# Two-layer transformer on one core: first-layer output products from split operands, reordered heads, later second-layer weights

## The chip, the cores and the metric

One core of one Trainium2 chip. The time is microseconds of device time from launch to end; of a kernel several executions are taken and the median stands for it. One more execution is profiled, and all rows come from that.

## What is computed

Two layers over 8 batches of 512 tokens with 128 features. In each layer attention and a feed-forward part both read the normalised rows, and both are added to the input. What matters here, cut from the reference:

```python
# layer 0, attention: 16 heads of 64 (x is normalised, 8 x 512 x 128)
y = jnp.einsum('bhcC,bhCv->bhcv', p, v)              # p: causal softmax
z = jnp.einsum('dvh,bhcv->bcd', W, y) * (math.sqrt(d_embed / d_value) / num_heads)
# layer 0, feed-forward: 32 routed experts (6 per token) and a shared one
hmid = jax.nn.silu(gate) * up
out = jnp.einsum('teh,te->th', y, combine) + shared_out
# layer 1, feed-forward: three blocks of two linear layers
w = q.astype(jnp.float32) / 7.5 - 1.0
w = w * jnp.repeat(scale, GROUP, axis=1)
base = jnp.einsum('btd,od->bto', x, w) + bias
lora = jnp.einsum('btr,or->bto', jnp.einsum('btd,rd->btr', x, la), lb)
return base + lora
```

## The kernel before

**Tiling.** Tokens of a batch are four tiles of 128; a product's moving operand has 512 columns. Many products are made in fp32r, a single-pass format: an operand is split in a high part (a rounded copy) and a low part (value minus high part), and `split_matmul` (lines 61 to 66) makes three products of them (high-high, high-low, low-high) in place of one fp32 product. Projections, scores, expert units and their down products are made so. The attention's output products (`project_out`, line 1703) are plain fp32 on `w_out0` and `yt`, eight per batch, one for each pair of heads, summed in PSUM bank 7 with the down products of the 17 units.

**Stages.** For batches 0 to 7: eight slots of attention, one for each pair of heads (`slot`, `score_group`), then 17 units (`units`: unit 0 is the shared expert, the others are two routed experts each). Within the units of batch b the rows, router logits, first projections and values of batch b + 1 are made. Where batch b's units end and batch b + 1's first slot begins stands `first_head`: the last down products, the output products of batch b and the first scores of batch b + 1. This stretch, up to the first turned blocks, is called a head below; there are seven, the first one after batch 0. After batch 7 comes layer 1 in two groups of four batches.

**A unit.** TensorE makes gate and up (bank pairs alternate), ScalarE the SiLU (`silu`, line 879), VectorE multiplies by the up half in PSUM (`gate`, line 1293; it frees the banks) and by the routing weights (`hidden`, line 1303, both operands in SBUF; the weights come by DMA to `crow`, three deep), ScalarE makes the high part (line 869), and VectorE (line 1297) or GpSimd (line 592) the low part (high part and value both in SBUF). For units 14, 15 and 16 it is VectorE. The down product of unit u follows the projection of unit u + 3. In batches 1 to 6 VectorE has layer 1's row statistics in unit 14.

**Other work of GpSimd.** `divide_pair` (line 588) multiplies `yt` by the inverse softmax sums, which SyncE fetches to `rrow` (two DMAs a pair). The two last pairs come behind the low part of unit 13. In batch 0, `second_layer_weights` dequantises layer 1's weights behind that.

**Order.** Each engine has its own queue, written out by hand; nothing is scheduled at run time but the semaphore waits. SyncE issues all DMAs from one queue, and waits in it for free buffers. The LoRA products (`add_lora`, line 1550) stand in unit 16 of batch 0; their operands are fetched in unit 2 of it, ScalarE copies them out of PSUM and GpSimd adds the rest.

Of the kernel before, what the change touches and what calls it, by code (L numbers as in the profile page):

```python
# [5 lines left out]
F32 = mybir.dt.float32  # L6
# [8 lines left out]
P = 128  # L15
# [8 lines left out]
R, GROUP, NLIN = 32, 16, 6  # L24
BLOCKS = NLIN // 2
# [56 lines left out]
def build(nc, a, out_dram):  # L82
    with ExitStack() as ctx:
# [17 lines left out]
        wqkv_rest = sb("wqkv_rest", [P, 2 * 3 * PAIRS * P - 2 * TILES * TILES * P])  # L101
        with ExitStack() as raw:
# [3 lines left out]
        w_out0 = sb("w_out0", [P, PAIRS, D])  # L106
# [11 lines left out]
        lin = sb("lin", [P, NLIN, D])  # L118
# [33 lines left out]
        rrow = sb("rrow", [P, RROWS, T])  # L152
        pt = sb("pt", [P, 2, TILES, TILES, P])
        yt = sb("yt", [P, PAIRS, T])
# [13 lines left out]
        hm_hi = [qk_hi[:, 1, 0, :], qk_hi[:, 1, 1, :], hm_third[:, 0, :]]  # L168
        hm_lo = [qk_lo[:, 1, 0, :], qk_lo[:, 1, 1, :], hm_third[:, 1, :]]
# [27 lines left out]


# [6 lines left out]
        la, lb = (flat_pt[0:R, k * NLIN * D:(k + 1) * NLIN * D].rearrange("p (n d) -> p n d", n=NLIN) for k in (0, 1))  # L205
        lora = lin[:, :, :].rearrange("p i o -> p (i o)")
# [106 lines left out]
        lora_taken = sem("lora_taken")  # L313
# [41 lines left out]
        y_divided = sem("y_divided")  # L355
        y_done = sem("y_done")
# [80 lines left out]
        SUMS_AFTER = [2, 3, 4, 8, 9, 10, 12, 13]  # L437
# [12 lines left out]
        LORA_AFTER = 16  # L450
# [14 lines left out]
        lora_loads = [(la, a["la"]), (lb, a["lb"])]  # L465
# [5 lines left out]
        def _(sp):  # L471
# [40 lines left out]
            for b in range(B):  # L512
# [6 lines left out]
                for u in range(2, UNITS):  # L519
# [4 lines left out]
                    if b == 0:  # L524
                        sp.wait_ge(y_done, PAIRS)
                        if u == 2:
                            for dst, src in lora_loads:
                                sp.dma_start(dst, src).then_inc(lora_loaded, 16)
                if b == 0:
                    sp.wait_ge(hm_ready, UNITS - 1)  # L530
                    sp.wait_ge(y_divided, PAIRS)
                    for dst, src in w1_loads:
                        sp.dma_start(dst, src).then_inc(w1_loaded, 16)
                    sp.wait_ge(lin_ready, 1)
# [10 lines left out]
        def _(pool):  # L545
# [58 lines left out]

            def split_gu(k):
# [18 lines left out]
            def second_layer_weights():  # L624
# [4 lines left out]
                setup.step(pool.tensor_tensor(wf, wf, qs, ALU.mult))  # L629
                pool.wait_ge(lora_taken, 2)  # L630
                pool.tensor_tensor(lin[:, :, :], lin[:, :, :], wf, ALU.add).then_inc(lin_ready, 1)
# [22 lines left out]
            for k in range(len(DOWN_PIECES)):  # L654
                split_down(k)
# [1648 lines left out]
```

## Time and profile before

| what | value |
|---|---|
| median of 3 runs | 1170.06 us (1169.66 to 1171.59) |
| the profiled execution | 1168.83 us |
| its span (first to last instruction) | 1167.0 us |
| busy: TensorE, VectorE, ScalarE, GpSimd | 99%, 85%, 70%, 35% |
| mean granted TensorE clock | 1.000 of full speed |
| chain that ended last | TensorE 87%, VectorE 6%, ScalarE 2% |
| fp32 output products (line 1703) | 61.6 us busy, 128 records of 603 ns (two for each product) |

How to read it: a timeline row has the start in us from the span's start, the duration, engine, line, operation, the tensor written, those read, and a count where rows were merged. Durations of TensorE overlap, since matmuls are pipelined: how fast it moves on is read from the distance of starts. A bracket gives the idle time before and what ended it.

### The profile page before, as it was taken

Reading aid. Unit: us, or ns where it says so; the run is one execution under the profiler, and the core shown is the slowest. Engines: PE = TensorE matmul, PEld = TensorE weight load, DVE = VectorE, ACT = ScalarE, POOL = GpSimd, SP = SyncE. Lnnn points to the kernel's source line nnn. Section 1 sums busy time; section 2 is a strip of 40 time slices with the busy share of each in tenths; the row PEclk is TensorE's granted clock in tenths of the full one; section 3 lists DMA queues with packets and bytes.
Section 4 is the critical chain, followed back from the end, with each engine's and each line's share of the span. In section 5 each row is a group of like instructions: output and inputs, shape, how many; then the busy total and the mean of one; then the engine's idle time right before and its main releaser. Section 6 shows DMA issues by size and latency. Waiting matters only on the chain.

```text
span 1167.0 us, 23979 instructions
## 1 busy us (share of the span) xinstructions
PE 1150.2 (99%) x8932; PEld 889.8 (76%) x8932; DVE 986.9 (85%) x1918; ACT 811.7 (70%) x2184; POOL 408.1 (35%) x365
## 2 busy tenths in 40 slices
PE   8999999999999999999999999999999999999998
PEld 6778778777776877677777777777778767777776
DVE  7988698979887989788888988898888778898897
ACT  6885677567756775677557765776577767877886
POOL 2326610730064006400550055005500577735741
PEclk9999999999999999999999999999999999999999
DMA  8014300410131003100320032003300330000001
GB/s 267 2 31 145 94 1 31 136 55 2 31 128 64 1 25 131 66 2 20 112 90 2 11 115 97 1 6 117 99 2 3 124 96 1 1 20 19 1 11 29
DMA packets 44565, 63.93 MB, mean 55 GB/s; under 512 B 8160, under 2 KB 18656, under 8 KB 44192
## 3 DMA queue, kind: packets, MB, share of 16 engines
q1 hardware_dynamic: 44448, 62.39, 16.6%
q8 instruction: 71, 1.16, 0.4%
q14 instruction: 46, 0.38, 0.1%
HBM read 59.48 MB, written 2.88 MB: 53 GB/s over the span
## 4 chain that ended last, share of the span: by engine, by line
PE 87%; DVE 6%; ACT 2%; issue 2%; POOL 1%; DMA 1%; SPq 0%; DVEq 0%; ACTq 0%; POOLq 0%
PE psum L1647 15%; PE psum L1666 13%; PE psum L1588 11%; PE psum L64 10%; PE psum L66 10%; PE psum L65 10%; PE psum L1703 5%; PE psum L1601 2%; PE psum L1613 2%; PE psum L1916 2%; PE psum L1670 1%; PE psum L1535 1%; PE psum L1972 1%; ACT probs L835 1%; DVE mneg L1247 1%
## 5 line engine op out<-in xcount | busy, mean ns | idle before, releaser
L793 ACT ACTIVATE probs<-psum,mneg 128x256 f32<-128x256 f32 (+3 forms) x400 | 187.3, 486 | 112.2 <-DVE mneg L1228 111.9
L1647 PE MATMUL psum<-ident,probs 128*128 128x128 f32 x1600 | 210.3, 276 | 3.6 <-ACT probs L835 3.4
L1228 DVE TENSOR_REDUCE mneg<-psum 128x2 f32<-128x1024 f32 (+3 forms) x256 | 194.1, 819 | 15.3 <-PE psum L1601 11.3
L1647 PEld LDWEIGHTS psum<-ident,probs 128*128 128x128 f32 x1600 | 178.0, 141 | 30.6 <-ACT probs L793 8.2
L1219 DVE COPY pt<-psum 128x512 f32<-128x512 f32 x256 | 164.9, 683 | 38.7 <-PE psum L1647 36.9
L592 POOL TENSOR_TENSOR qk_lo<-sg,qk_hi 128x512 fp32r<-128x512 f32 x64 | 91.7, 1438 | 155.5 <-ACT qk_hi L869 155.5
L1666 PE MATMUL psum<-pt,v_all 128*64 128x384 f32 (+5 forms) x1088 | 142.6, 412 | 0.0
L556 POOL TENSOR_TENSOR rstd<-var,mhalf 128x4 f32<-128x4 f32 x7 | 7.1, 1012 | 385.6 <-DVE var L1112 385.6
L1666 PEld LDWEIGHTS psum<-pt,v_all 128*64 128x64 f32 (+1 forms) x1088 | 69.7, 135 | 62.7 <-issue 50.2
L64 PE MATMUL psum<-xt_hi,gu_hi 128*128 128x512 f32 x272 | 110.2, 405 | 0.0
L66 PE MATMUL psum<-xt_hi,gu_lo 128*128 128x512 f32 x272 | 107.7, 396 | 0.0
L588 POOL TENSOR_TENSOR yt<-yt,rrow 128x512 f32<-128x512 f32 x64 | 98.9, 1551 | 24.5 <-DMA rrow<-sums 24.4
L65 PE MATMUL psum<-xt_lo,gu_hi 128*128 128x512 f32 x272 | 107.3, 394 | 0.0
L1303 DVE TENSOR_TENSOR sg<-sg,crow 128x512 f32<-128x512 f32 x88 | 98.3, 1117 | 7.8 <-DMA crow<-weights 5.0
L879 ACT ACTIVATE sg<-psum 128x512 f32<-128x512 f32 x96 | 57.0, 595 | 48.7 <-PE psum L66 48.6
L1588 PE MATMUL psum<-qk_hi 64*128 64x256 f32 (+3 forms) x512 | 88.5, 342 | 0.2 <-DVE v_all L1288 0.2
L1208 DVE SCALAR_TENSOR_TENSOR qk_lo<-psum,qk_hi 128x512 fp32r<-128x512 f32 x72 | 49.7, 690 | 44.5 <-ACT qk_hi L816 44.4
L793 ACT ACTIVATION_READ_ACCUMULATOR probs<-psum,mneg 128x1 f32 x400 | 83.6, 209 | 0.0
L1588 PE MATMUL psum<-qk_hi,qk_lo 64*128 64x256 f32 (+3 forms) x512 | 82.3, 318 | 0.0
L1588 PE MATMUL psum<-qk_lo,qk_hi 64*128 64x256 f32 (+3 forms) x512 | 82.3, 318 | 0.0
L869 ACT ACTIVATE qk_hi<-sg 128x512 fp32r<-128x512 f32 x96 | 60.3, 628 | 28.3 <-DVE sg L1303 28.1
L1293 DVE TENSOR_TENSOR sg<-sg,psum 128x512 f32<-128x512 f32 x96 | 65.2, 680 | 17.3 <-ACT sg L879 17.0
(294 smaller groups left out, 2762.3 us busy)
## 6 DMA issues: line engine op xcount, KB each, us to landing
crow<-weights SPq DMA_DIRECT2D x256, 128.0 KB, 2.9
rrow<-sums SPq DMA_DIRECT2D x128, 128.0 KB, 3.0
gu_raw<-in_gu SPq DMA_DIRECT2D x1, 2176.0 KB, 12.4
x_all<-in_x SPq DMA_DIRECT2D x8, 256.0 KB, 5.5
out_rows<-x_all SPq DMA_DIRECT2D x7, 256.0 KB, 2.3
down_raw<-in_down SPq DMA_DIRECT2D x1, 1088.0 KB, 13.0
wqkv_raw<-in_wqkv SPq DMA_DIRECT2D x1, 768.0 KB, 6.1
wqkv_raw<-in_wqkv SPq DMA_DIRECT2D x1, 512.0 KB, 5.1
```

What stands on the lines that cost most here:

```text
L64: nc.tensor.matmul(out, lh, rh, start=start, stop=False, **kw)
L65: nc.tensor.matmul(out, lh, rl, start=False, stop=False, **kw)
L66: return nc.tensor.matmul(out, ll, rh, start=False, stop=stop, **kw)
L588: pool.tensor_tensor(yt[:, p, :], yt[:, p, :], rrow[:, n % RROWS, :], ALU.mult).then_inc(y_divided, 1)
L592: pool.tensor_tensor(hm_lo[u % 3], sg[u % 3], hm_hi[u % 3].bitcast(F32), ALU.subtract).then_inc(pool_lo_ready, 1)
L793: last = act.activation(probs[:, h * HALF + PROB[t]:h * HALF + PROB[t] + w], bank[score_bank(rnd, c) + h][:, o:o + w], ACT.Exp, bias=mneg[ ...
L1219: dve.tensor_copy(pt[:, s % 2, :, 3 - s // 2, :], turn_bank(rnd, s).rearrange("p (j q) -> p j q", q=P)).then_inc(pt_ready, 1)
L1228: last = dve.tensor_reduce(mneg_h[:, :, t], psum[:, b:b + 2, o:o + P * (t + 1)], AX, ALU.max, negate=True)
L1303: dve.tensor_tensor(sg[u % 3], sg[u % 3], crow[:, m % CROWS, :], ALU.mult).then_inc(hm_ready, 1)
L1588: ins = mm(bank[score_bank(rnd, c) + h][:, o:o + w], ql[r, 0, qs_], kl[r, 1, ks], start=i == 0 and n == 0 and not masked, stop=masked, **K)
L1647: last = nc.tensor.transpose(dst[:, i * P:(i + 1) * P], probs[:, v:v + P], ident[:, :])
L1666: last = mm(Y[c:c + m, first * P:T], v(k), rows_t[:, k, first:TILES, :].rearrange("p t q -> p (t q)"), start=(k == 0), stop=(k == TILES - ...
```

## The change

- **Output products.** For batches 0 to 6 `project_out` is made from split operands: 24 fp32r products in place of 8 fp32 ones. ScalarE makes the high parts of the rows (`high_rows`, from unit 10 to 16), GpSimd the low parts (`low_rows`, all eight behind its last division). The weight is split in batch 0, and joined again to fp32 in batch 7 for that batch's products, which stay plain.
- **Head.** The output products stand behind the first two chunks of the next batch's scores and all down products. Two come before the rest of the first slot's scores, two behind. Projections, down products and the masks change places; on ScalarE and VectorE the orders follow. The three buffers of the units' high and low parts are rotated.
- **Sums.** The inverse sums of the last two pairs are fetched one unit earlier.
- **Second layer's weights.** They are dequantised behind batch 6's units and not behind batch 0's. The LoRA products go from unit 16 of batch 0 to unit 6 of batch 7, as two products in each of three row groups, with six DMAs in place of two; VectorE adds them to the weights straight from PSUM.

```diff
-        SUMS_AFTER = [2, 3, 4, 8, 9, 10, 12, 13]
+        SUMS_AFTER = [2, 3, 4, 8, 9, 10, 11, 12]
+
+        HIGH_ROWS = {10: [0], 11: [1], 12: [2], 13: [3], 14: [4], 15: [5], 16: [6, 7]}
...
-                    if b == 0:
-                        sp.wait_ge(y_done, PAIRS)
-                        if u == 2:
-                            for dst, src in lora_loads:
-                                sp.dma_start(dst, src).then_inc(lora_loaded, 16)
...
+                    if b == B - 1 and u == 2:
+                        sp.wait_ge(y_done, ROUNDS0)
+                        for dst, src in lora_loads:
+                            sp.dma_start(dst, src).then_inc(lora_loaded, 16)
...
+            def low_rows(b):
+
+                for p in range(PAIRS):
+                    pool.wait_ge(yt_hi_ready, b * PAIRS + p + 1)
+                    pool.tensor_tensor(yt_lo[p], yt[:, p, :], yt_hi[p].bitcast(F32), ALU.subtract).then_inc(yt_lo_ready, 1)
+
+            def split_w_out0():
+                pool.wait_ge(w_out0_hi_ready, 1)
+                setup.step(pool.tensor_scalar(w_out0[:, :, :], w_out0[:, :, :], OUT0, None, ALU.mult))
+                pool.tensor_tensor(w_out0_lo[:, :, :], w_out0[:, :, :], w_out0_hi[:, :, :].bitcast(F32), ALU.subtract).then_inc(w_out0_lo_ready, 1)
+
+            def join_w_out0():
+
+                pool.wait_ge(acc_done, B - 1)
+                pool.tensor_tensor(w_out0[:, :, :], w_out0_lo[:, :, :].bitcast(F32), w_out0_hi[:, :, :].bitcast(F32), ALU.add).then_inc(w_out0_whole, 1)
...
-                if b == 0:
+                if b < B - 1:
+                    low_rows(b)
+                if 0 < b < B - 1:
+                    inv_sqrt1(b - 1)
+                if b == B - 2:
+                    join_w_out0()
                     second_layer_weights()
-                elif b < B - 1:
-                    inv_sqrt1(b - 1)
...
+            def high_rows(b, p):
+
+                act.wait_ge(y_divided, b * PAIRS + p + 1)
+                act.activation(yt_hi[p], yt[:, p, :], ACT.Copy).then_inc(yt_hi_ready, 1)
...
+            def add_lora():
+
+                dve.wait_ge(wf_ready, 1)
+                dve.wait_ge(lora_done, 1)
+                tiles = lin.rearrange("p (j k) d -> p k j d", k=LORA_TILES)
+                products = psum[:, 4:4 + LORA_TILES, 0:2 * D].rearrange("p k (j d) -> p k j d", d=D)
+                dve.tensor_tensor(tiles, tiles, products, ALU.add).then_inc(lin_ready, 1)
...
                     if p == 0 and b:
+                        row_maxima(n, 0)
                         rest_q(n + 1, SCALE0)
                         rest_k(n + 1)
-                        row_maxima(n, 0)
...
             def project_out(b, i):
-                pe.wait_ge(y_divided, b * PAIRS + 2 * i + 2)
+                pe.wait_ge(yt_lo_ready, b * PAIRS + 2 * i + 2)
+                for p in (2 * i, 2 * i + 1):
+                    last = split_matmul(nc, ACC, (w_out0_hi[:, p, :], w_out0_lo[:, p, :]), (yt_hi[p], yt_lo[p]), False, p == PAIRS - 1, **K)
+                return last
...
                 elif b:
+                    project_out(b - 1, 2)
                     project_out(b - 1, 3).then_inc(acc_done, 1)
```

On TensorE, the head behind batch 0, from unit 13's down product on. Before (`yt`, `w_out`: the output products; `down`: down products; `wqkv`: projections; `hide`, `later`: masks), with the rest of the down products and the projections behind the last row here:

```order
L64 MATMUL psum<-qk_hi,down_hi 128x512 [waits pool_lo_ready]
L65 MATMUL psum<-qk_lo,down_hi 128x512
L66 MATMUL psum<-qk_hi,down_lo 128x512
L1703 MATMUL psum<-yt,w_out 128x512 [waits y_divided,act_setup]
L1703 MATMUL psum<-yt,w_out 128x512
L64 MATMUL psum<-hm_third,down_hi 128x512 [waits lo_ready]
L65 MATMUL psum<-hm_third,down_hi 128x512
L66 MATMUL psum<-hm_third,down_lo 128x512
L1703 MATMUL psum<-yt,w_out 128x512 [waits y_divided]
L1703 MATMUL psum<-yt,w_out 128x512
```

After, the same start, and then the end of the down products:

```order
L65 MATMUL psum<-hm_third,down_hi 128x512 [waits pool_lo_ready]
L66 MATMUL psum<-hm_third,down_hi 128x512
L67 MATMUL psum<-hm_third,down_lo 128x512
L65 MATMUL psum<-xt_hi,wqkv_hi 128x512 [waits v_taken,w_out0_lo_ready]
L66 MATMUL psum<-xt_lo,wqkv_hi 128x512
L67 MATMUL psum<-xt_hi,wqkv_lo 128x512
L65 MATMUL psum<-qk_hi,down_hi 128x512 [waits lo_ready]
L66 MATMUL psum<-qk_lo,down_hi 128x512
L67 MATMUL psum<-qk_hi,down_lo 128x512
```

```order
L65 MATMUL psum<-hm_third,down_hi 128x512 [waits lo_ready]
L66 MATMUL psum<-hm_third,down_hi 128x512
L67 MATMUL psum<-hm_third,down_lo 128x512
L65 MATMUL psum<-rows_hi,w_out_hi 128x512 [waits yt_lo_ready]
L66 MATMUL psum<-rows_lo,w_out_hi 128x512
L67 MATMUL psum<-rows_hi,w_out_lo 128x512
```

The output products left the place ahead of the last three down products (units 14 to 16) and stand behind them; the down product of unit 14 has one projection ahead of it and no output products.

On GpSimd, the end of batch 1's units (`rrow`: divisions, `hm_third`: a unit's low part, `rstd` and `nmr`: statistics). Before:

```order
L588 TENSOR_TENSOR yt<-yt,rrow 128x512 [waits y_ready,rrow0_loaded1]
L592 TENSOR_TENSOR qk_lo<-sg,qk_hi 128x512 [waits hi_ready]
L588 TENSOR_TENSOR yt<-yt,rrow 128x512 [waits y_ready,rrow0_loaded2]
L588 TENSOR_TENSOR yt<-yt,rrow 128x512 [waits y_ready,rrow0_loaded0]
L637 TENSOR_TENSOR rstd<-var,mhalf 128x4 [waits x1_var_ready]
```

After:

```order
L604 TENSOR_TENSOR yt<-yt,rrow 128x512 [waits y_ready,rrow0_loaded1]
L608 TENSOR_TENSOR hm_third<-sg,hm_third 128x512 [waits hi_ready]
L604 TENSOR_TENSOR yt<-yt,rrow 128x512 [waits y_ready,rrow0_loaded2]
L604 TENSOR_TENSOR yt<-yt,rrow 128x512 [waits y_ready,rrow0_loaded0]
L625 TENSOR_TENSOR rows_lo<-yt,rows_hi 128x512 [waits yt_hi_ready] x8
L668 TENSOR_TENSOR rstd<-var,mhalf 128x4 [waits x1_var_ready]
```

Eight operations of 512 columns came in between the last division and the statistics.

On SyncE, unit 2 of batch 7 after the change (`rrow`: inverse sums, `crow`: routing weights):

```order
L527 DMA rrow<-sums 64x512 [waits y_divided]
L527 DMA rrow<-sums 64x512
L544 DMA pt<-in_la 32x2x128 [waits y_done]
L544 DMA pt<-in_la 32x2x128 x2
L544 DMA pt<-in_lb 32x2x128 x3
L515 DMA crow<-weights 64x512 [waits hm_ready]
L515 DMA crow<-weights 64x512
```

Before, the two `crow` DMAs followed the two `rrow` DMAs at once; the six of the LoRA operands came in between.

## Rows read from the trace of the kernel before

**Rows 1.** The page, part 1: busy us (share of the span) xinstructions.

```profile
PE 1150.2 (99%) x8932; PEld 889.8 (76%) x8932; DVE 986.9 (85%) x1918; ACT 811.7 (70%) x2184; POOL 408.1 (35%) x365
```

**Rows 2.** Timeline of TensorE, second head: start us, us, engine, line, op, tiles.

```profile
246.27 1.88 PE L1703 MATMUL psum<-yt,w_out 128*128 128x512 f32 x4
...
248.22 0.40 PE L65 MATMUL psum<-hm_third,down_hi 128*128 128x512 f32 x1
...
251.09 0.39 PE L64 MATMUL psum<-qk_hi,down_hi 128*128 128x512 f32 x1
...
252.92 0.40 PE L66 MATMUL psum<-xt_hi,wqkv_lo 128*128 128x512 f32 x1
253.25 0.34 PE L1601 MATMUL psum<-hide,later 64*128 64x64 bf16 x8
...
255.09 1.98 PE L1703 MATMUL psum<-yt,w_out 128*128 128x512 f32 x4
257.00 0.38 PE L1588 MATMUL psum<-qk_hi 64*128 64x256 f32 x2
...
258.38 1.98 PE L1703 MATMUL psum<-yt,w_out 128*128 128x512 f32 x4
260.20 1.47 PE L1647 MATMUL psum<-ident,probs 128*128 128x128 f32 x12
```

**Rows 3.** Timelines of GpSimd and VectorE, units 9 and 10 of batch 1.

```profile
224.45 3.47 POOL L588 TENSOR_TENSOR yt<-yt,rrow 128x512 f32<-128x512 f32 x2
...
225.69 1.08 DVE L1303 TENSOR_TENSOR sg<-sg,crow 128x512 f32<-128x512 f32 x1
226.69 1.78 DVE L1297 TENSOR_TENSOR hm_third<-probs,hm_third 128x512 fp32r<-128x512 f32 x1
```

**Rows 4.** Timelines of GpSimd and VectorE before and in that head.

```profile
241.22 3.02 POOL L588 TENSOR_TENSOR yt<-yt,rrow 128x512 f32<-128x512 f32 x2
...
244.96 0.69 DVE L1303 TENSOR_TENSOR sg<-sg,crow 128x512 f32<-128x512 f32 x1
245.57 0.69 DVE L1297 TENSOR_TENSOR hm_third<-probs,hm_third 128x512 fp32r<-128x512 f32 x1
...
247.13 0.69 DVE L1303 TENSOR_TENSOR sg<-sg,crow 128x512 f32<-128x512 f32 x1
247.74 1.48 DVE L1297 TENSOR_TENSOR qk_lo<-sg,qk_hi 128x512 fp32r<-128x512 f32 x2
```

**Rows 5.** Timeline of ScalarE, unit 16 of the second batch.

```profile
245.77 0.60 ACT L879 ACTIVATE sg<-psum 128x512 f32<-128x512 f32 x1 [1.39 <-PE psum L66]
```

**Rows 6.** Timelines: last division of batch 3, multiply of unit 15 in batch 0.

```profile
480.22 1.51 POOL L588 TENSOR_TENSOR yt<-yt,rrow 128x512 f32<-128x512 f32 x1 [1.27 <-DMA rrow<-sums]
...
124.41 0.69 DVE L1303 TENSOR_TENSOR sg<-sg,crow 128x512 f32<-128x512 f32 x1
```

**Rows 7.** The page, part 5: busy us, mean ns of one | idle before, releaser.

```profile
L1303 DVE TENSOR_TENSOR sg<-sg,crow 128x512 f32<-128x512 f32 x88 | 98.3, 1117 | 7.8 <-DMA crow<-weights 5.0
```

**Rows 8.** Timeline of TensorE, end of batch 0.

```profile
126.43 1.60 PE L1550 MATMUL psum<-pt 32*128 32x128 f32 x12
127.96 0.50 PE L64 MATMUL psum<-qk_hi,down_hi 128*128 128x512 f32 x1
```

**Rows 9.** Timeline of TensorE, last projection of unit 6 in batch 7.

```profile
922.86 0.40 PE L66 MATMUL psum<-xt_hi,gu_lo 128*128 128x512 f32 x1
```

**Rows 10.** Timeline of SyncE's DMA issues: batch 7, then the scales in batch 0.

```profile
919.56 1.23 SPq L510 DMA_DIRECT2D rrow<-sums  x2
...
129.63 3.67 SPq L533 DMA_DIRECT2D crow<-in_qs  x8
```

**Rows 11.** DMA issues: count, KB each, median us to landing.

```profile
crow<-in_qs SPq DMA_DIRECT2D x8, 48.0 KB, 2.6
...
pt<-in_lb SPq DMA_DIRECT2D x1, 96.0 KB, 3.0
```

**Rows 12.** Timeline of GpSimd, last step of the dequantised weights.

```profile
147.57 1.82 POOL L631 TENSOR_TENSOR lin<-lin,crow 128x768 f32<-128x768 f32 x1
```

More of the change, by code:

```diff
@@ L24 @@
 R, GROUP, NLIN = 32, 16, 6
+LORA_TILES = 3
 BLOCKS = NLIN // 2
@@ L105, in build @@
         down_hi = sb("down_hi", [P, UNITS, D], F32R)
-        w_out0 = sb("w_out0", [P, PAIRS, D])
+        w_out0_hi = sb("w_out0_hi", [P, PAIRS, D], F32R)
+        with ExitStack() as raw:
+            w_out0 = raw.enter_context(nc.sbuf_tensor("w_out0", [P, PAIRS, D], F32))
+        w_out0_lo = sb("w_out0_lo", [P, PAIRS, D], F32R)
         with ExitStack() as raw:
@@ L152, in build @@
         rrow = sb("rrow", [P, RROWS, T])
+        with ExitStack() as rows:
+            rows_hi = rows.enter_context(nc.sbuf_tensor("rows_hi", [P, PAIRS, T], F32R))
         pt = sb("pt", [P, 2, TILES, TILES, P])
+        with ExitStack() as rows:
+            rows_lo = rows.enter_context(nc.sbuf_tensor("rows_lo", [P, PAIRS, T], F32R))
         yt = sb("yt", [P, PAIRS, T])
@@ L196, in build @@
         flat_yt = yt[:, :, :].rearrange("p n t -> p (n t)")
+        yt_hi, yt_lo = ([v[:, p, :] for p in range(PAIRS)] for v in (rows_hi, rows_lo))
         flat_crow = crow[:, :, :].rearrange("p n t -> p (n t)")
@@ L204, in build @@
         bias_raw = flat_rrow[:, 0:NLIN * D].rearrange("p (n d) -> p n d", n=NLIN)
-        la, lb = (flat_pt[0:R, k * NLIN * D:(k + 1) * NLIN * D].rearrange("p (n d) -> p n d", n=NLIN) for k in (0, 1))
-        lora = lin[:, :, :].rearrange("p i o -> p (i o)")
+        la, lb = (pt1[0:LORA_TILES * R, 0, 0, 2 * k:2 * k + 2, :] for k in (0, 1))
         room = [v_all[:, :, :].rearrange("p t n -> p (t n)"), room0[:, :], room1[:, :], flat_yt]
@@ L355, in build @@
         y_divided = sem("y_divided")
+        w_out0_hi_ready = sem("w_out0_hi_ready")
+        w_out0_lo_ready = sem("w_out0_lo_ready")
+        w_out0_whole = sem("w_out0_whole")
+        yt_hi_ready = sem("yt_hi_ready")
+        yt_lo_ready = sem("yt_lo_ready")
         y_done = sem("y_done")
@@ L464, in build @@
         W_LOADS = 16 * len(late_loads)
-        lora_loads = [(la, a["la"]), (lb, a["lb"])]
+        lora_loads = [(v[r * R:(r + 1) * R, :, :], a[n].rearrange("r (j k) d -> k r j d", k=LORA_TILES)[r, :, :, :])
+                      for v, n in ((la, "la"), (lb, "lb")) for r in range(LORA_TILES)]
         w1_loads = [(qw, a["qw"]), (bias_raw, a["bias_row"].partition_broadcast(P))]
@@ L628, in second_layer_weights @@
                 setup.step(pool.tensor_scalar(wf, wf, 1.0 / 7.5, -1.0, ALU.mult, ALU.add))
-                setup.step(pool.tensor_tensor(wf, wf, qs, ALU.mult))
-                pool.wait_ge(lora_taken, 2)
-                pool.tensor_tensor(lin[:, :, :], lin[:, :, :], wf, ALU.add).then_inc(lin_ready, 1)
+                pool.wait_ge(v_done, B * FILLS)
+                pool.tensor_tensor(lin, wf, qs, ALU.mult).then_inc(wf_ready, 1)
             def inv_sqrt1(b):
@@ L654, in _ @@
             for k in range(len(DOWN_PIECES)):
+                if k == 1:
+                    split_w_out0()
                 split_down(k)
@@ L944, in first_layer @@
                             take_values(b + 1, range(2 * (u - V_AFTER), 2 * (u - V_AFTER) + 2))
-                        if b == 0 and u == LORA_AFTER:
+                        for p in HIGH_ROWS.get(u, []):
+                            high_rows(b, p)
+                        if b == 0 and u == W1_AFTER:
                             second_layer_weights()
@@ L1547, in add_lora @@
                 pe.wait_ge(lora_loaded, 16 * len(lora_loads))
-                o = psum[:, 4:6, :].rearrange("p b n -> p (b n)")
-                for i in range(NLIN):
-                    last = mm(o[:, i * D:(i + 1) * D], la[:, i, :], lb[:, i, :], start=True, stop=True)
+                pe.wait_ge(rinv0_copied, B)
+                pe.wait_ge(y_ready, ROUNDS0)
+                for j in range(NLIN // LORA_TILES):
+                    for i in range(LORA_TILES):
+                        r = slice(i * R, (i + 1) * R)
+                        last = mm(bank[4 + i][:, j * D:(j + 1) * D], la[r, j, :], lb[r, j, :], start=True, stop=True)
                 last.then_inc(lora_done, 1)
```

83 lines of the change are left out of this document (41 added, 42 removed).

## The prediction

> **What bounds the kernel now.** First the page's busy shares: TensorE is at work for 99% of the span [rows 1], so the order of the first layer is set by its queue, and a product that is shortened there counts whole unless TensorE then waits. Next its timeline where the second batch ends and the third begins, which I call a head [rows 2]; then the timelines of VectorE and GpSimd over the same microseconds [rows 3, 4], since the change gives both more to do or something else to meet; last the DMA queue. TensorE has no gap in a head. In [rows 4] VectorE has 0.69 to 0.74 us for each low part and each product with the routing weights, since GpSimd has by then only four-column work left.
>
> Three things are to be seen in the rows. (a) A product with an fp32r pair moves on every 0.23 us: nine of them from 251.09 to 252.92 and a step [rows 2]. (b) A pair of fp32 output products (four records) holds TensorE from 246.27 to 248.22 less one step, so 1.72 us [rows 2]. The pairs beside the narrow score products take 1.8 to 1.9 us. (c) GpSimd and VectorE do not overlap when a VectorE operation reads two tensors in SBUF. In [rows 3] GpSimd has two divisions back to back, 3.47 us in place of some 2.5. VectorE's multiply beside them takes 1.08 us and the low part behind it 1.78, against 0.69 when alone. Their ends, 226.77 and 228.47, are 1.70 us apart: one GpSimd operation (about 1.2 us) and one of VectorE (0.5), turn about.
>
> **The output products, if nothing is late.** I count a head from 246.27, where the down product of unit 13 is done; before, it ends at 260.20, where the turned blocks start: 13.93 us [rows 2]. After: 6 projection, 9 down and 24 output products are 39 x 0.23 = 9.0 us; the masks and the first two chunks of scores take 1.84 us now (253.25 to 255.09) and about 0.1 more since the masks are split; third chunk, next first chunk and masks take 1.38 us now (257.00 to 258.38), 0.05 less behind a short product; three changes between wide and narrow products are some 0.1 each, as between 252.92 and 253.25. Sum 12.5, a gain of 1.4 us. Seven heads would give 9.8 us.
>
> **What the low parts do to it.** The gain needs GpSimd to make eight low parts (line 625 of the changed kernel) behind its last division. That ends at 244.24 [rows 4], so they run from there, in the very microseconds in which VectorE multiplies and splits units 15 and 16. They are about 1.25 us each, so ten microseconds without a pause; the ScalarE copies that feed them are ready in time. ScalarE itself idles 1.39 us before the SiLU of unit 16 [rows 5], as before those of the units with value copies; that covers a copy of 0.6 us in each.
>
> Now VectorE's five operations, one by one, at the pace of 1.70 us per turn, where before they ended at 245.6, 246.26, 247.8, 248.5 and 249.2 [rows 4]. The first low row holds the port until 245.5: multiply 15 ends at 246.0, low part 14 at 247.75, the gate of unit 16 (one operand in PSUM, so I take it as not held up) at 248.4, multiply 16 at 249.5, low part 15 at 251.2, low part 16 at 252.9. TensorE in the new order wants low part 14 at 247.0: it waits 0.8. Projection and the first scores then bring it to 251.2, where low part 15 is just there. Unit 16's down product, wanted at 251.1 in the undelayed order, starts at 253.0. So a head loses 1.9 us and gains 1.4: **0.5 us longer**. Of what stands behind it nothing more is late: the low rows are done at about 257, the fourth output pair begins at 259; maxima, rests and exponentials of the first scores are done by 257.
>
> In batches 2 to 6 the last division now starts later; in batch 3 it waits 1.27 us for its rows and is done at 481.73 [rows 6], 0.5 us before the head's first output product. The change fetches those rows one unit earlier, which puts the same ten microseconds of work at the same place. So six heads at +0.45 are +2.7 us. In the first head VectorE has no row statistics in unit 14: it multiplies unit 15 at 124.41 [rows 6], 1.9 us before the end of unit 16's projection and not 0.6 as in the second, so the whole chain is about 1.1 us earlier: wait 0.7 in place of 1.85, that is -0.7. Heads together: **+2.0 us**. Bounds: -9.8, if no operation waits, and +1.0 per head (+7), if each VectorE operation meets a whole GpSimd operation. I take the middle chain since it is the pattern of [rows 3], which recurs wherever GpSimd has two operations in a row.
>
> Averages would tell otherwise: if each of the five took only what line 1303 takes on average, 1117 ns [rows 7], low part 16 would end at 249.2 + 5 x 0.43 = 251.35 and a head would be 1.1 us shorter. The Trainium skill (SBUF — State Buffer, Who interferes with whom) has the shared port pair as an exclusive lock, held for a whole instruction, also against a VectorE instruction with two SBUF inputs; by that rule, which speaks against this change, the delay comes whole, as in the chain above and in [rows 3], and the heads are +2.0 and not -7.7 us.
>
> **The LoRA products.** Removed from batch 0: twelve records from 126.43 to 127.96, with changes of width 126.34 to 128.07 [rows 8]: **-1.7 us** on TensorE. The two copies of ScalarE there (0.58 and 0.38 us) were covered. In batch 7 the products follow unit 6, whose last product starts at 922.86, so TensorE is there at 923.1 [rows 9]. Their operands come by six DMAs that SyncE issues behind the row loads of 919.56, so from 920.8 on [rows 10]. A DMA issue takes 0.46 us (eight in 3.67) to 0.61 us (two in 1.23); the last issue starts between 923.1 and 923.9. Landing takes 2.6 us (48 KB) to 3.0 us (96 KB) [rows 11], so 925.7 to 926.9: TensorE waits 2.6 to 3.8 us, and I take 3.2. Behind the six are the routing weights of unit 6 and later units; they land about 3 us later, no more than TensorE has been delayed, so that isn't paid twice. The products: three row groups at once, 0.5 us, up to the 1.5 of before, with changes of width 0.7. VectorE's addition of 768 columns, about 1 us, fits, since TensorE wants the next gate, that of unit 7, only for unit 9, two units on. Batch 7: **+3.9 us** (3.2 to 5.4).
>
> **The rest.** The dequantised weights (bias parts, casts, multiplies) ran beside the first slots of batch 1 until 149.4 [rows 12], before its routing. Now they stand behind low rows, statistics and the joined output weight, and last until the second slot of batch 7's routing, whose multiplies also read two SBUF tensors: 0 to 1.8 us, one such operation [rows 12]; I take **+0.5**, nearer to nothing, since few meet. SyncE waits for them before batch 7's weights, an attention stage later: nothing. The splitting of the output weight in batch 0, about 3 us of GpSimd, lies between low parts that wait for ScalarE: nothing, with a margin of a slot. The last batch keeps its fp32 products.
>
> **Sum:** 2.0 - 1.7 + 3.9 + 0.5 = +4.7 us on 1168.83 of the profiled execution, 1173.5; the median of the runs is 1.2 above that execution, so 1174.7.
>
> **Rivals.** (1) *The port costs nothing* or only the average: heads -9.8 or -7.7 us, with the LoRA wait +2.2: 1162.4 to 1164.5. For it: VectorE has time to spare in a head, since its five operations were through by 249.2 and the new order wants the last of them at 251.1. Against: they are delayed by 3.7 us, not by two, and low part 14 is wanted at once. 0.2. (2) *The operands land in time*, as if issues were quicker or units 2 to 5 ran later: -3.2, so 1171.5, no measurable change. For it: in batch 0 the two loads delayed the routing weights by a microsecond at no cost to TensorE. Against: TensorE now waits for the transfers themselves. With middle cases of the port, 0.2. (3) *Slower still*: each VectorE operation meets a whole one of GpSimd (+5), batch 7's wait is 5.4 in place of 3.9, routing +1.5: 1182.7. It decides from the point where low part 16 ends later than 253.4. TensorE's granted clock is full over the span, and TensorE has no wait of 3 us in it; what such a wait does to the clock no row shows. If it fell to 1.2 GHz for one unit, that is 2 us more. The Trainium skill (TensorE: Matmul & The Clock Gate, Part 1) has an idle array returned to the lower clock; no run here shows it. 0.15. (4) *The forecast*, heads a little longer and a wait in batch 7: 0.45.
>
> **How the numbers follow.** Forecast 1174.7. The range 1162.5 to 1181.0 leaves out the far ends of (1) and (3). Faster by over 0.2% (2.3 us, about what a measurement can tell) is under 1167.7: case (1) with a part of the middle, 0.23. Within it, to 1172.4: 0.2. Slower: 0.57.
>
> **What would show it.** TensorE waits some 0.8 us for low part 14 and a microsecond for low part 16 in heads 2 to 7; VectorE's low parts there take 1.7 us, not 0.69; the output products take 1.4 us a pair; a head lasts 14.4 us, and less in the first; before the LoRA products TensorE waits about 3 us for a DMA. It is wrong if the low rows don't start until the low parts are through, if low parts stay at 0.7 us, or if the wait in batch 7 is missing.

## The result and the profile after

The changed kernel takes **1178.41 us** (median of 6 runs, 1175.91 to 1180.63); the kernel before, on the same chip, 1169.28 us (6 runs, 1168.54 to 1171.59). The ratio is 1.008, 95% interval 1.0069 to 1.009: slower by 9.1 us. The profiled execution of it took 1175.91 us, with a span of 1174.1 us, 7.1 more than the 1167.0 before; it is the shortest of the six.

I call the moment at which the projection of unit 16 ends T (read as the start of the product behind it), and read how long each stretch lasts from TensorE's timeline:

| stretch, us | before | after | difference | forecast |
|---|---|---|---|---|
| seven heads, T to the first turned block, without the LoRA products | 7 x 14.63 | 14.04, 15.24, 15.28, 14.31, 15.25, 15.27, 15.27 | +2.3 | +2.0 |
| LoRA products in batch 0 | 1.73 | - | -1.7 | -1.7 |
| batch 7's attention, first turned block to its units | 57.38 | 58.32 | +0.9 | +0.5 |
| batch 7's units up to T | 40.31 | 45.68 | +5.4 | +3.9 |
| everything else | | | +0.2 | 0 |

First the second head, as TensorE sees it. T is 243.71 here (245.57 before). A timeline's columns are start, duration, engine, line, operation, tiles, count; a bracket gives the idle time before and what ended it. Compare with [rows 2].

```profile
244.88 0.40 PE L67 MATMUL psum<-xt_hi,wqkv_lo 128*128 128x512 f32 x1
245.90 0.50 PE L65 MATMUL psum<-qk_hi,down_hi 128*128 128x512 f32 x1 [0.63 <-DVE qk_lo L1339]
...
249.98 0.40 PE L67 MATMUL psum<-qk_hi,down_lo 128*128 128x512 f32 x1
250.99 0.50 PE L65 MATMUL psum<-hm_third,down_hi 128*128 128x512 f32 x1 [0.60 <-DVE hm_third L1339]
...
251.78 0.39 PE L65 MATMUL psum<-rows_hi,w_out_hi 128*128 128x512 f32 x1
...
253.18 0.40 PE L65 MATMUL psum<-rows_hi,w_out_hi 128*128 128x512 f32 x1
```

Three single-pass products make up one fp32 product, and the six of the next pair begin 1.40 us after the first (1.72 before), as forecast. But TensorE now has two gaps, one ahead of unit 14's down product and one ahead of unit 16's, both for a low part that VectorE makes. From start to start they last 1.02 and 1.01 us where a step is 0.23, and the product behind each takes a step of 0.33 to 0.34 us: 0.9 us lost at each, of which the brackets show 0.63 and 0.60 as idle time. In the view of the waits (total, times, longest, in us) these and the wait of batch 7 lead:

```profile
PE psum L65 <- DVE hm_third L1339: 3.9, 7, 0.6
PE psum L65 <- DVE qk_lo L1339: 3.5, 6, 0.7
PE psum L1605 <- DMA pt<-in_lb: 3.5, 1, 3.5
```

Timelines of VectorE and of GpSimd in that head:

```profile
243.06 1.09 DVE L1345 TENSOR_TENSOR sg<-sg,crow 128x512 f32<-128x512 f32 x1
244.07 1.78 DVE L1339 TENSOR_TENSOR qk_lo<-probs,qk_hi 128x512 fp32r<-128x512 f32 x1
...
246.48 1.06 DVE L1345 TENSOR_TENSOR sg<-sg,crow 128x512 f32<-128x512 f32 x1
247.47 1.77 DVE L1339 TENSOR_TENSOR qk_lo<-sg,qk_hi 128x512 fp32r<-128x512 f32 x1
249.16 1.77 DVE L1339 TENSOR_TENSOR hm_third<-sg,hm_third 128x512 fp32r<-128x512 f32 x1
...
242.29 12.29 POOL L625 TENSOR_TENSOR rows_lo<-yt,rows_hi 128x512 fp32r<-128x512 f32 x8
```

The same five operations of VectorE stand in [rows 4] with 0.69 to 0.74 us each. Together they take 7.47 us, some 4.0 longer, and all of it lies beside the eight low rows of GpSimd, where GpSimd had been through with its last division.

Batch 7 has the other loss. SyncE, then TensorE:

```profile
920.79 1.23 SPq L527 DMA_DIRECT2D rrow<-sums  x2
922.06 2.55 SPq L544 DMA_DIRECT2D pt<-in_la  x3
924.66 1.87 SPq L544 DMA_DIRECT2D pt<-in_lb  x3
...
924.10 0.40 PE L67 MATMUL psum<-xt_hi,gu_lo 128*128 128x512 f32 x1
928.04 1.13 PE L1605 MATMUL psum<-pt 32*128 32x128 f32 x12 [3.54 <-DMA pt<-in_lb]
929.10 0.80 PE L65 MATMUL psum<-qk_hi,down_hi 128*128 128x512 f32 x1
929.69 0.63 PE L66 MATMUL psum<-qk_lo,down_hi 128*128 128x512 f32 x1
930.12 0.63 PE L67 MATMUL psum<-qk_hi,down_lo 128*128 128x512 f32 x1
...
931.73 0.40 PE L65 MATMUL psum<-xt_hi,gu_hi 128*128 128x512 f32 x1
```

The last issue of an operand starts at about 925.9 (three of 0.62 us from 924.66), when TensorE had already been ready for a microsecond and a half. Behind the wait of 3.54 us the single-pass products start 0.43 us apart and not 0.23, until 931.4. That is TensorE at the lower of its two clocks, 1.2 GHz. The busy times by stretch say the same (columns: length, busy time of each engine, then the granted clock, the share of the DMA engines, GB/s):

```profile
925.00:930.00 5.00, 1.96 (x14) 1.64 (x15) 1.16 (x2) 0.93 (x2) 2.49 (x3) 0.82 0.39 104
930.00:935.00 5.00, 5.00 (x22) 3.98 (x22) 3.26 (x4) 2.36 (x6) 1.17 (x1) 0.84 0.65 200
```

The smaller loss is in batch 7's attention. There GpSimd is still at the second layer's weights when VectorE comes to the routing in the second slot, and an operation that took 0.29 us before takes 1.69:

```profile
858.24 1.64 POOL L653 TENSOR_TENSOR rrow<-rrow,bias_bf 32x768 f32<-32x768 f32 x1
...
858.35 1.69 DVE L1206 TENSOR_TENSOR corr<-rl,ebias 128x128 f32<-128x128 f32 x1
```

### The profile page after: what moved, and what is told of

It reads as the page before. It is cut to its first block, busy times and chain, and to the rows that moved or that the text cites. A ratio compares the mean times of both kernels' runs of the same rounds, so it can differ in the third digit from the quotient of the medians.

```text
span 1174.1 us, 24220 instructions
## 1 busy us (share of the span) xinstructions
PE 1146.1 (98%) x8988; PEld 898.8 (77%) x8988; DVE 1020.5 (87%) x1919; ACT 838.3 (71%) x2238; POOL 494.5 (42%) x423
## 3 DMA queue, kind: packets, MB, share of 16 engines
q8 instruction: 71, 1.16, 0.4%
## 4 chain that ended last, share of the span: by engine, by line
PE 70%; DVE 20%; issue 4%; ACT 3%; DMA 1%; SPq 1%; POOL 0%; DVEq 0%; ACTq 0%; POOLq 0%
PE psum L1702 14%; PE psum L1721 12%; PE psum L1643 10%; PE psum L65 7%; PE psum L67 6%; PE psum L66 6%; DVE sg L1345 3%; DVE probs L1345 3%; DVE qk_lo L1339 3%; DVE sg L1335 3%; PE psum L1656 2%; PE psum L1668 2%; PE psum L1975 2%; DVE probs L1335 1%; PE psum L1725 1%
## 5 line engine op out<-in xcount | busy, mean ns | idle before, releaser
L1261 DVE COPY pt<-psum 128x512 f32<-128x512 f32 x256 | 165.0, 684 | 46.2 <-PE psum L1702 44.4
L1345 DVE TENSOR_TENSOR sg<-sg,crow 128x512 f32<-128x512 f32 x88 | 103.6, 1177 | 8.0 <-DMA crow<-weights 5.3
L608 POOL TENSOR_TENSOR qk_lo<-sg,qk_hi 128x512 fp32r<-128x512 f32 x32 | 48.2, 1505 | 95.0 <-ACT qk_hi L907 95.0
L625 POOL TENSOR_TENSOR rows_lo<-yt,rows_hi 128x512 fp32r<-128x512 f32 x56 | 86.0, 1569 | 0.0
L836 ACT ACTIVATE probs<-psum,mneg 128x512 f32<-128x512 f32 x112 | 77.7, 720 | 0.3 <-issue 0.2
```

Source lines behind the costliest of these rows:

```text
L1261: dve.tensor_copy(pt[:, s % 2, :, 3 - s // 2, :], turn_bank(rnd, s).rearrange("p (j q) -> p j q", q=P)).then_inc(pt_ready, 1)
L1345: dve.tensor_tensor(sg[u % 3], sg[u % 3], crow[:, m % CROWS, :], ALU.mult).then_inc(hm_ready, 1)
```

## The experiments

My theory had two parts: (a) GpSimd's low rows hold up VectorE's operations that read two tensors in SBUF, and this costs a head more than the cheaper products give; (b) the late LoRA operands cost the wait and, behind it, the clock. The rivals: the new order itself costs time, the low parts are late for a reason of ScalarE, and the clock falls for another reason. All medians below stand against runs of the kernel before on the same chip, 1169.1 to 1169.7 us.

**Operands early.**

```diff
+                if b == B - 1:
+                    sp.wait_ge(qk_done, 2 * ROUNDS0)
+                    for dst, src in lora_loads:
+                        sp.dma_start(dst, src).then_inc(lora_loaded, 16)
                 store_weights(b)
...
-                    if b == B - 1 and u == 2:
-                        sp.wait_ge(y_done, ROUNDS0)
-                        for dst, src in lora_loads:
-                            sp.dma_start(dst, src).then_inc(lora_loaded, 16)
```

> The changed kernel, with the six DMAs for the LoRA operands issued by SyncE ahead of batch 7's routing weights (behind the last projection of batch 7, which frees their place) and not behind unit 2's loads. Nothing is left out. Theory (the operand wait in batch 7 costs 3.5 us and halves the granted clock for about a unit): the wait before the LoRA products is gone, the granted clock stays at 1.00 in 925 to 935 us, batch 7's units last 41.4 us and not 45.68, and the time falls by 4 to 7 us, to 1171 to 1174. Rival A (only the wait counts, the lower clock is made up by later waits): -3.5 us at most, 1175. Rival B (TensorE then waits for the second layer's weights or for a bank instead): no change, 1178.

Measured: 1173.33 us (4 runs, 1172.52 to 1176.43), 1.0041 of before (1.0025 to 1.0057). Batch 7's units last 40.50 us, against 45.68. On TensorE's timeline the LoRA products have no idle time ahead of them:

```profile
926.97 0.72 PE L1605 MATMUL psum<-pt 32*128 32x128 f32 x12
```

And the clock is full (busy times by stretch):

```profile
925.00:930.00 5.00, 5.00 (x31) 3.81 (x30) 3.62 (x5) 3.48 (x8) 3.71 (x3) 1.00 0.61 180
930.00:935.00 5.00, 5.00 (x25) 4.04 (x25) 4.89 (x6) 4.22 (x9) 3.71 (x4) 1.00 0.58 189
```

So the place of six DMA issues in SyncE's queue is worth 5.2 us, and the LoRA products themselves only 0.2 over the 40.31 of before, less than the 0.7 they hold TensorE: the kernel before had two short waits for low parts in that stage, 0.9 us together, and this one has a single wait of 0.4. These are the waits of the kernel before (895 to 945 us):

```profile
PE psum L64 <- DVE hm_third L1297: 0.5, 1, 0.5
PE psum L64 <- POOL hm_third L592: 0.4, 1, 0.4
```

Theory (b) held, and rivals A and B fell. The heads are as in the changed kernel, but for that of batch 3, 15.29 us against 14.31.

**The wait kept, but filled.**

```diff
+                for _ in range(14):
+                    mm(bank[4][:, 0:P], ident[:, :], ident[:, :], start=True, stop=True)
                 pe.wait_ge(lora_loaded, 16 * len(lora_loads))
```

> The changed kernel, with 14 fp32 products of 128 columns (into a bank that is overwritten later, about 3 us) ahead of the wait for the LoRA operands in batch 7. Nothing is left out; the wait ends when it did. Theory (the idle wait itself brings the granted clock down): clock 1.00 in 925 to 935 us, the products behind the wait move on every 0.23 us from the first, and the time falls by 1.5 to 2.5 us. Rival (the clock falls for another reason): it still falls, and the time stays or rises by up to 0.5 us.

Measured: 1176.08 us (4 runs, 1173.84 to 1177.8), 1.0059 of before (1.0041 to 1.0077). The units last 43.99 us, 1.7 less than 45.68. TensorE's timeline, then its clock (1.00) in the stretch behind:

```profile
927.19 3.29 PE L1602 MATMUL psum<-ident 128*128 128x128 f32 x28
930.77 0.72 PE L1607 MATMUL psum<-pt 32*128 32x128 f32 x12 [0.30 <-DMA pt<-in_lb]
```

```profile
930.00:935.00 5.00, 4.70 (x32) 3.74 (x31) 2.01 (x3) 1.18 (x3) 1.67 (x2) 1.00 0.55 180
```

With e1 this splits batch 7's 5.4 us: 3.5 for the wait (43.99 less 40.50), 1.7 for the clock, 0.2 for the products. That the idle wait brought the clock down is shown by this pair: same wait, TensorE at work in it, no drop. The 1.7 is the difference of two profiled executions; how long the clock stays down differs between executions, as the next kernel shows.

**No low rows.** The third product reads the high part in their place, so the output lacks the low part of the rows.

```diff
-                if b < B - 1:
-                    low_rows(b)
...
-                pe.wait_ge(yt_lo_ready, b * PAIRS + 2 * i + 2)
+                pe.wait_ge(yt_hi_ready, b * PAIRS + 2 * i + 2)
...
-                    last = split_matmul(nc, ACC, (w_out0_hi[:, p, :], w_out0_lo[:, p, :]), (yt_hi[p], yt_lo[p]), False, p == PAIRS - 1, **K)
+                    last = split_matmul(nc, ACC, (w_out0_hi[:, p, :], w_out0_lo[:, p, :]), (yt_hi[p], yt_hi[p]), False, p == PAIRS - 1, **K)
```

> The changed kernel without GpSimd's eight low rows per batch: the third product of each output pair reads the high part in their place, so TensorE has the same number of products and VectorE and ScalarE the same work, but the first layer's attention output isn't the reference's. Theory (GpSimd's subtractions hold the port that VectorE's two-operand operations need): VectorE's low parts of units 14 and 16 take 0.69 us and not 1.78, TensorE's waits of 0.6 us for each are gone, heads 2 to 7 last 13.2 to 14.0 us from the end of unit 16's projection to the first turned block (15.25 now), the time falls by 8 to 13 us, to 1165 to 1170. Rival (the low parts are late for another reason, such as ScalarE's two copies of rows in unit 16): they end where they end now, and the time stays within 2 us of 1178.

Measured: 1167.85 us (10 runs, 1165.87 to 1168.45), 0.9986 of before (0.9977 to 0.9996), and that with the wait of batch 7 still in it (3.26 us). Behind that wait ten steps in a row are 0.43 us in its profiled execution, against four in the changed kernel's, and batch 7's units last 46.2 us:

```profile
920.88 0.63 PE L66 MATMUL psum<-qk_lo,down_hi 128*128 128x512 f32 x1
...
925.15 0.51 PE L67 MATMUL psum<-hm_third,down_lo 128*128 128x512 f32 x1
```

All seven heads last 13.47 us. VectorE in the second head (T is 244.49):

```profile
243.86 0.69 DVE L1343 TENSOR_TENSOR sg<-sg,crow 128x512 f32<-128x512 f32 x1
244.47 0.69 DVE L1337 TENSOR_TENSOR qk_lo<-probs,qk_hi 128x512 fp32r<-128x512 f32 x1
...
246.66 0.68 DVE L1337 TENSOR_TENSOR qk_lo<-sg,qk_hi 128x512 fp32r<-128x512 f32 x1
247.44 0.69 DVE L1337 TENSOR_TENSOR hm_third<-sg,hm_third 128x512 fp32r<-128x512 f32 x1
```

ScalarE's two copies in unit 16 are still there, so that rival fell, and theory (a) held. The low rows cost a usual head 1.8 us (15.27 less 13.47), and the first 0.6.

**Plain fp32 products in the new order.**

```diff
-                    last = split_matmul(nc, ACC, (w_out0_hi[:, p, :], w_out0_lo[:, p, :]), (yt_hi[p], yt_lo[p]), False, p == PAIRS - 1, **K)
+                    last = mm(ACC, w_out0[:, p, :], yt[:, p, :], start=False, stop=(p == PAIRS - 1), **K)
```

High rows, low rows, the split and the join of the weight are gone too.

> The changed kernel in its new order of the head, but with plain fp32 output products in all batches: no high rows, no low rows, no split weight. Nothing is left out. Theory (the new order by itself costs nothing, the low rows do): no waits of TensorE for low parts in the head, and heads of 14.6 us (the fp32 pair costs 1.72 us, the split one 1.40; before, a head took 14.63), so five heads 0.6 us shorter, the first 0.6 longer: 1175 to 1177, since the wait in batch 7 stays. Rival (the order costs time, whatever the format): heads of 15.2 us or more, 1178 or above.

Measured: 1174.95 us (4 runs, 1173.41 to 1175.6), 1.0046 of before (1.0029 to 1.0063). All heads last 14.76 us, 0.13 more than before. So the order costs 0.1 us a head, the split products give 1.3 (14.76 less 13.47), and the low rows take 1.8. It had something I hadn't asked for: batch 7's attention is back at 57.38 us, since without low rows and join GpSimd was through with the second layer's weights earlier.

**Which operations of GpSimd.** Each low row is made by two operations of one operand.

```diff
-  pool.tensor_tensor(yt_lo[p], yt[:, p, :], yt_hi[p].bitcast(F32), ALU.subtract).then_inc(yt_lo_ready, 1)
+  setup.step(pool.tensor_scalar(yt_lo[p], yt_hi[p].bitcast(F32), 0.0, None, ALU.mult))
+  pool.tensor_scalar(yt_lo[p], yt_hi[p].bitcast(F32), 0.0, None, ALU.mult).then_inc(yt_lo_ready, 1)
```

> The changed kernel with each low row made by two GpSimd operations of one operand (the high row times zero, twice, one behind the other), about as long as the subtraction, which reads two. The products are the same in number, but the low part of the attention output is left out of the result. Theory (what holds VectorE up is a GpSimd operation with two operands in SBUF): VectorE's low parts of units 14 and 16 take 0.69 us beside them, heads 13.5 us, time near e2_no_low_rows (1168). Rival (any long GpSimd operation holds the port): they take 1.2 to 1.8 us, heads 14.5 to 15.3 us, time 1173 to 1178.

Measured: 1259.47 us (4 runs, 1258.45 to 1260.4), far outside both expectations. I had taken the two together to last as long as one subtraction, but each takes 1.49 us, so eight rows take 24 us, and TensorE waits for them (view of the waits):

```profile
PE psum L65 <- POOL rows_lo L626: 60.9, 21, 4.4
```

The time says nothing on the question, then; the timelines of GpSimd and VectorE in the second head do:

```profile
255.69 1.50 POOL L625 TENSOR_SCALAR rows_lo<-rows_hi 128x512 fp32r<-128x512 f32 x1
257.27 1.82 POOL L626 TENSOR_SCALAR rows_lo<-rows_hi 128x512 fp32r<-128x512 f32 x1
259.05 1.60 POOL L625 TENSOR_SCALAR rows_lo<-rows_hi 128x512 fp32r<-128x512 f32 x1
...
256.44 0.69 DVE L1346 TENSOR_TENSOR sg<-sg,crow 128x512 f32<-128x512 f32 x1
257.05 0.69 DVE L1340 TENSOR_TENSOR qk_lo<-probs,qk_hi 128x512 fp32r<-128x512 f32 x1
...
259.22 1.10 DVE L1340 TENSOR_TENSOR qk_lo<-sg,qk_hi 128x512 fp32r<-128x512 f32 x1
```

Beside one-operand operations of GpSimd, VectorE's five take 3.85 us together, against 7.47 in the changed kernel and 3.44 without low rows. Of VectorE's rows above, the first (256.44) lies wholly within GpSimd's of 255.69 and still takes 0.69. Four other heads also sum to 3.85. The first and the fourth come to 4.73 and 4.46, and in these VectorE's first operation still meets the last division. So the subtraction costs much more than the one-operand operation. That its second operand is the reason fits, but isn't shown alone, since the two are different operations and last 1.25 and 1.49 us.

**The low rows taken out of the meeting.** From here on I looked for a kernel that beats both. On top of the early operands; the second table gives the low rows that follow the division of pair 3, 4 and 5:

```diff
-        HIGH_ROWS = {10: [0], 11: [1], 12: [2], 13: [3], 14: [4], 15: [5], 16: [6, 7]}
+        HIGH_ROWS = {10: [0], 11: [1, 2], 12: [3], 13: [4], 14: [5], 16: [6, 7]}
+        LOW_ROWS = {3: [0], 4: [1], 5: [2, 3]}
...
+                pool.wait_ge(lo_ready, (b + 1) * (UNITS - len(POOL_LO)))
+                for p in range(4, PAIRS):
+                    low_row(b, p)
```

> e1_early_lora with the low rows taken out of the head's contention: GpSimd makes the rows 0 to 3 between its divisions in units 9 to 11 (their high parts come a unit or two earlier on ScalarE), and the rows 4 to 7 behind VectorE's last low part. Nothing is left out. Theory (only the meeting of the low rows with VectorE's two-operand operations in units 15 and 16 costs the head): all seven heads 13.5 us as in e2_no_low_rows (15.27 now), no wait of TensorE for low parts, so 11 us less than e1's 1173.3: 1162 to 1163. Rival A (the port time is only moved): VectorE falls behind in units 10 to 12 and TensorE waits there, up to 1.3 us per batch, units 46.7 us instead of 45.4 to 46.0: 1169 to 1171. Rival B (the rows 4 to 7 come too late): TensorE waits before the third output pair, heads over 14.5 us.

Measured: 1167.98 us (12 runs, 1164.69 to 1170.39), 0.9986 of before (0.9976 to 0.9996). Half of what I expected: four heads of 14.53 to 14.56 us and one of 14.45, not 13.5; only the first (13.60) and the sixth (13.71) come near. Units lasted as before, so rival A fell. The next kernel shows why.

**GpSimd's order behind batch 6.**

```diff
+                if b == B - 2:
+                    second_layer_weights()
                 if 0 < b < B - 1:
                     inv_sqrt1(b - 1)
                 if b == B - 2:
                     join_w_out0()
-                    second_layer_weights()
```

> e4_both, with GpSimd's order behind batch 6's units changed: second-layer weights, then the statistics' roots, then the joined output weight. Nothing is left out. Theory (batch 7's attention is 0.9 to 1.0 us longer because the last of the weights' conversions meets VectorE's routing): in e5_plain_fp32, where they begin at 845.4, it is back at 57.38 us; here it is 57.4 to 57.9 and the time 0.5 to 1.0 us under e4_both. Rival (the joined weight or the last multiplication meets the routing instead): 58.4 us or more, no gain.

Measured: 1165.75 us (5 runs, 1163.81 to 1167.6), 0.9965 of before (0.9952 to 0.9978). Batch 7's attention is 57.38 us, 1.0 less than in e4, as expected; the median fell by 2.2, and the rest of that is not explained. The first head lasts 13.47 us and the others 14.50 to 14.56. The timelines of GpSimd, VectorE and TensorE in the second tell what is late:

```profile
241.84 2.99 POOL L605 TENSOR_TENSOR yt<-yt,rrow 128x512 f32<-128x512 f32 x2
...
242.60 1.08 DVE L1354 TENSOR_TENSOR sg<-sg,crow 128x512 f32<-128x512 f32 x1
243.60 1.77 DVE L1348 TENSOR_TENSOR qk_lo<-probs,qk_hi 128x512 fp32r<-128x512 f32 x1
...
245.43 0.50 PE L65 MATMUL psum<-qk_hi,down_hi 128*128 128x512 f32 x1 [0.81 <-DVE qk_lo L1348]
```

The rows 2 and 3 had pushed the two last divisions back, and now those met VectorE.

**Two rows early, six late.**

```diff
-        LOW_ROWS = {3: [0], 4: [1], 5: [2, 3]}
+        LOW_ROWS = {3: [0], 4: [1]}
...
-                for p in range(4, PAIRS):
+                for p in range(2, PAIRS):
```

> e7_both_weights_first with the low rows 2 and 3 not ahead of the two last divisions but, with 4 to 7, behind VectorE's last low part. Nothing is left out. Theory (in e7 the two last divisions came 2.5 us later and met the multiplication of unit 15 and low part 14, 1.08 and 1.77 us, so TensorE still waited 0.8 us a head): the divisions are back by unit 14, low part 14 takes 0.69 us, heads 2 to 7 last 13.5 us and not 14.55, the six late low rows end 11.2 us behind the end of unit 16's projection and are wanted at 12.1; the time is 5 to 6.5 us under e7's 1165.75, 1159 to 1161. Rival A (the last low rows are late): TensorE waits before the last output pair, heads 14 us or more, 1163. Rival B (low parts are held up by something other than GpSimd's operations): heads stay at 14.5 us, 1165 to 1166.

Measured: **1161.5 us** (5 runs, 1160.56 to 1162.7), 0.9932 of before (0.9918 to 0.9945). All seven heads last 13.47 us, with no wait for a low part. GpSimd, then VectorE (T is 243.05):

```profile
246.77 7.52 POOL L613 TENSOR_TENSOR rows_lo<-yt,rows_hi 128x512 fp32r<-128x512 f32 x6 [4.92 <-DVE hm_third L1348]
...
243.18 0.68 DVE L1348 TENSOR_TENSOR qk_lo<-probs,qk_hi 128x512 fp32r<-128x512 f32 x1
```

Alone, a low row takes 1.25 us and not 1.5. But batch 7's attention is at 58.54 us again. The last multiplication of the weights now began just before a small one of VectorE's routing:

```profile
847.46 1.87 POOL L670 TENSOR_TENSOR wqkv_rest<-crow 128x768 f32<-128x768 f32 x1
...
847.49 2.00 DVE L1214 TENSOR_TENSOR rl<-rexp,route_sum 128x128 f32<-128x128 f32 x1
```

**That multiplication behind the routing.**

```diff
                 pool.wait_ge(v_done, B * FILLS)
+                pool.wait_ge(qk_done, 2 * ((B - 1) * PAIRS + 4))
```

> e10_two_early with GpSimd's last multiplication of the second-layer weights (768 columns, two operands in SBUF, 1.87 us) made to wait until TensorE has the projections of batch 7's fourth pair, that is until VectorE's multiplication in the routing of its second slot is through. Nothing is left out. Theory (this one meeting costs batch 7's attention 1.1 us: VectorE's 0.29 us multiplication took 2.00 us beside it in e10, and TensorE waited 0.9 us for VectorE's copy behind it): the multiplication is back at 0.29 us, batch 7's attention at 57.4 us and not 58.54, the time 1.0 to 1.3 us under e10: 1160.3. Rival (the joined output weight or the roots behind it now meet a routing operation): the wait is only moved, 58.4 us or more, 1161.5.

Measured: **1160.05 us** (5 runs, 1159.21 to 1161.3), 0.9919 of before (0.9905 to 0.9932). Batch 7's attention is 57.36 us, and the two operations no longer meet:

```profile
850.87 1.88 POOL L671 TENSOR_TENSOR wqkv_rest<-crow 128x768 f32<-128x768 f32 x1 [2.93 <-PE psum L67]
...
847.78 0.29 DVE L1215 TENSOR_TENSOR rl<-rexp,route_sum 128x128 f32<-128x128 f32 x1
```

So the idea of the change was worth 9.3 us; as it was placed, it cost 9.1.

## Why the prediction came out as it did

The direction was right, and so was the port as the mechanism of the heads; the sum was short: +4.7 us were forecast on the profiled execution, +7.1 came, and +9.1 between the medians.

- **The output products, if nothing is late.** Forecast: a head of 13.2 us from T (12.5 and the 0.7 up to the down product of unit 13) and a gain of 1.4. Shown by the kernel without low rows: 13.47, a gain of 1.16. The pair's 1.40 us was exact; the sum was 0.27 short. The new order takes 0.13 of that (plain products, 14.76 against 14.63). The step that I rounded to 0.23 is 0.233 (six in 1.40), about 0.12 over 39 products.
- **What the low parts do to it.** Forecast 1.9 us for a head by stepping VectorE's five operations one by one; measured 1.8. Low part 14 was to end at T + 2.2 and ended at T + 2.1; low part 16 at T + 7.3, and it was T + 7.2. I had the two waits at 0.8 us and 1.1 (from 251.9 to 253.0 in the chain); by the starts each came out at 0.9. By the mean of the page [rows 7] a head would have become shorter.
- **The first head and batch 3.** The first: -0.7 forecast, -0.6 measured. In batch 3 I saw no difference from the others; it came out at 14.31, as there TensorE didn't wait for low part 14. In e1 this head took 15.29 like the rest, so it is a matter of the execution. Heads together +2.3, forecast +2.0.
- **Second layer's weights.** Forecast 0.5 of a range up to 1.8; measured 0.9. I had named the routing's multiplications as the possible meeting. It was there, but the operation hit was the addition behind them (line 1206), also with both operands in SBUF: 0.29 us became 1.69, and TensorE waited 0.73 us for the copy behind it. The multiplication took 0.45 in place of 0.29. Before, TensorE had no wait between 845 and 910 us. I took the small value because few operations would meet; one was enough.
- **The LoRA products.** The wait was sized at 3.2 (2.6 to 3.8) from the places of the issues in SyncE's queue and was 3.54. That it fits is in part luck, since two errors cancel: from the first issue to the start of the last it took 3.8 us and not 2.3 to 3.1 (the first three take 0.85 us each), and the last operand landed 2.1 us behind its issue, not 2.6 to 3.0. The step that failed is the term behind the wait. I had the fall of the clock to 1.2 GHz as a part of the third rival, 2 us, and left it out of the sum; it came and cost 1.7 (e3 against the changed kernel), and more in e2's profiled execution. The Trainium skill (TensorE: Matmul & The Clock Gate, Part 1), named there, has an idle array returned to the lower clock; the trace agrees, with 0.43 us from product to product behind the wait of 3.54 us. The products' own 0.7 was right, but shorter waits for low parts gave back 0.5 of it. The 5.4 us of batch 7 equal the upper end of my range by chance: I had reached it with the longest wait and slow products, not with the clock.
- **From the profiled execution to the median.** I added the 1.2 us of before. For the changed kernel the median lies 2.5 us above its profiled execution. One part is seen: in e1 the first projections are still at the lower clock (0.42 us apart up to 11 us) and batch 0's units start at 82.18 us, not 80.92. Executions of e3, e5 and e10 also have a granted clock of 0.97 between 1000 and 1060 us, where the changed kernel's and e1's have 1.00. The result has the mean granted clock of each of the six executions of the changed kernel: 0.998 in the shortest (the profiled one), 0.999 in the two of 1177.6 us, 0.997 at 1179.3 and 0.995 in the two of 1180.6. My estimate: 0.995 over 1178.8 us is 5.9 us of clock missing, 0.998 over 1174.1 is 2.3, so most of the 4.7 us between these executions can be the clock. The two at 0.999 must be longer for another reason, such as the start. Where in these executions the clock fell isn't shown, so some 2 us of the 9.1 stay open.

Rival 1, in which the port costs nothing, was right on what the products are worth and wrong on the price; its heads appear once the meeting is gone (e10). Rival 2, operands in time, was put at 1171.5 and measures 1173.3 when it is brought about (e1).

## What to carry to other kernels

Before work is moved to GpSimd, list the VectorE operations with two SBUF operands in the same microseconds and step through them in turn; their mean says nothing, and a meeting of one 0.3 us operation can reach TensorE. Work that is wanted late belongs behind such operations, and what is pushed back by it has to be looked at again (e4). A transfer for work that is moved is to be issued where its place in memory comes free, not where the work stands, since a wait of 3.5 us of TensorE was paid here with half as much again at the lower clock.

## What was not expected of the hardware

- How much VectorE is held up depends on GpSimd's operation. Beside two-operand subtractions of GpSimd a VectorE low part took 1.77 us; beside one-operand multiplications, which read SBUF too, 0.68 to 1.10. The Trainium skill (SBUF — State Buffer, Who interferes with whom) lets any GpSimd instruction that reads SBUF contend with such a VectorE operation, with the loser blocked for the whole instruction; e8 differs: one VectorE operation lay wholly within such an instruction and took its usual 0.69 us, and none was lengthened by more than 0.4 beside instructions of 1.5 us. GpSimd's own stretched from 1.50 to 1.82 there.
- GpSimd's one-operand multiplication of 128x512 with an fp32r result took 1.49 us, more than the subtraction with two operands (1.25 alone). The dequantisation's form, two steps on 768 columns in fp32, took 0.83.
- In e10 a 0.29 us operation of VectorE that began 0.03 us behind a long one of GpSimd lasted until that one was done: 2.00 us beside 1.87.
- In e8, where TensorE waits for low rows in every head (3.47, 0.67 and 3.13 us in the second), the granted clock is 0.63 of full from 270 to 283 us, and 0.966 over the span.
